# Linear recurrence stage: gate weights multiplied with the input weights beforehand, phases counted in turns, sums made by TensorE, all in two halves

## The reference, cut to what matters

```python
def _L2_attn_a_ref(x, w_in, b_in, w_gx, b_gx, w_ga, b_ga, a_real_param, a_imag_param, w_out, b_out):
    xh = x @ w_in + b_in                               # 128 -> 256 channels
    gate_x = sigmoid(_bdl(xh, w_gx, b_gx))             # block diagonal, 256 -> 128
    gate_a = sigmoid(_bdl(xh, w_ga, b_ga))
    log_a = -8.0 * gate_a * softplus(a_real_param)
    log_a_imag = a_imag_param * gate_a
    a = exp(complex(log_a, log_a_imag))
    xc = complex(xh[..., :128], xh[..., 128:])
    xc = gate_x * xc
    norm = sqrt(maximum(1.0 - exp(2.0 * log_a), 1e-06))
    xc = norm * xc
    h = associative_scan(h_t = a_t * h_{t-1} + xc_t)   # along the sequence
    y = concatenate([h.real, h.imag], -1) @ w_out + b_out
x = x + _L2_attn_a_ref(_layernorm(x), ...)
```

## Time and profile before

| | us |
|---|---|
| median of 3 runs | 2849.07 |
| lowest, highest | 2848.08, 2852.46 |
| the profiled execution's own time | 2850.44 |
| its span, first to last instruction | 2848.7 |
| busy: PE, DVE, ACT, POOL | 2286.7, 1795.9, 1416.0, 690.6 |
| mean granted TensorE clock (share of full speed) | 0.887 |
| this stage, first instruction to the next stage's first | 1896.04 to 2002.92 |

### The profile page before, as it was taken

One profiled execution on the slowest core, in us unless ns is written; L12 is line 12 of the kernel. 1 busy time (PEld: TensorE's weight loads), 2 busy tenths in 40 slices (PEclk: granted clock), 3 DMA queues, 4 the chain that ended last, 5 costly groups with the idle time before them and its releaser, 6 DMA issues. The chain is left out here.

```text
span 2848.7 us, 41029 instructions
## 1 busy us (share of the span) xinstructions
PE 2286.7 (80%) x14474; PEld 1486.8 (52%) x14474; DVE 1795.9 (63%) x4001; ACT 1416.0 (50%) x3610; POOL 690.6 (24%) x448
## 2 busy tenths in 40 slices
PE   7999998887988797898655878780777889698977
PEld 4555554563664365464335776340332667475647
DVE  4655555884874795794655664338346899546863
ACT  4444544673773585584531214652553766315750
POOL 0000000561650362461022430000000779123000
PEclk9999998999999998998867989895887999878996
DMA  1000001010100210110102320000000122100010
GB/s 44 9 10 11 11 11 61 22 27 16 23 20 5 75 24 12 27 24 8 46 9 53 73 51 17 11 11 0 6 13 32 60 75 74 63 10 1 2 62 16
DMA packets 79015, 80.17 MB, mean 28 GB/s; under 512 B 28624, under 2 KB 63952, under 8 KB 77808
## 3 DMA queue, kind: packets, MB, share of 16 engines
q1 hardware_dynamic: 78832, 77.80, 9.5%
HBM read 53.55 MB, written 8.52 MB: 22 GB/s over the span
## 5 line engine op out<-in xcount | busy, mean ns | idle before, releaser
L800 ACT ACTIVATE window_s<-window_s,window_soft 128x128 f32<-128x128 f32 x512 | 197.7, 394 | 5.0 <-DVE window_soft L963 5.0
L878 POOL TENSOR_TENSOR window_pa<-window_pa,window_pb 128x1024 f32<-128x1024 f32 x64 | 151.6, 2369 | 152.3 <-DVE window_pb L945 152.3
L870 POOL TENSOR_TENSOR window_s<-window_s,window_soft 128x512 f32<-128x512 f32 x128 | 133.2, 1041 | 219.8 <-DVE window_soft L900 219.6
L963 DVE CUSTOM_DVE_ANT_0 window_s<-ps,window_mask,window_nrn 128x128 f32<-128x128 f32 x512 | 148.5, 346 | 46.6 <-PE ps L645 29.9
L2854 DVE TENSOR_TENSOR_SCAN mamba_bx<-ps,mamba_ab 128x256 f32<-128x256 f32 x256 | 154.5, 667 | 18.8 <-PE ps L2640 18.8
L608 PE MATMUL ps<-window_wa,window_sh 128*128 128x512 f32 x256 | 132.1, 641 | 41.6 <-DVE window_pb L945 29.0
L861 POOL MEMSET window_sh<- 64x2048 f32 x2 | 3.6, 1800 | 569.8 <-POOLq L53 569.8
L3024 ACT ACTIVATE rope_p<-ps,rope_mx 128x128 f32<-128x128 f32 (+1 forms) x256 | 104.3, 419 | 48.7 <-DVE rope_mx L3078 48.7
L2637 PE MATMUL ps<-mamba_m,mamba_xt 128*128 128x129 f32 x512 | 103.0, 283 | 29.4 <-ACT mamba_m L2712 20.6
L100 ACT ACTIVATE ln_sq<-ps 128x512 f32<-128x512 f32 x120 | 71.5, 597 | 106.1 <-PE ps L83 105.3
L83 PE MATMUL ps<-x,consts 128*128 128x512 f32 x128 | 84.4, 821 | 49.4 <-PEq L53 38.2
(11 more groups left out here) (577 smaller groups left out, 6235.1 us busy)
## 6 DMA issues: line engine op xcount, KB each, us to landing
mamba_cbr<-mamba_c SPq DMA_DIRECT2D x32, 512.0 KB, 3.6
window_vs<-window_vt SPq DMA_DIRECT2D x64, 128.0 KB, 2.3
delta_xi<-delta_x SPq DMA_DIRECT2D x16, 512.0 KB, 4.7
switch_w<-in_switch_w SPq DMA_DIRECT2D x4, 2048.0 KB, 10.2
window_wa<-in_window_wa SPq DMA_DIRECT2D x4, 1152.0 KB, 7.3
linattn_wb<-in_linattn_wb SPq DMA_DIRECT2D x6, 513.0 KB, 3.5
window_wb<-in_window_wb SPq DMA_DIRECT2D x4, 537.5 KB, 8.2
window_sh<-y SPq DMA_DIRECT2D x16, 128.0 KB, 2.2
```

Source lines behind the costliest of these rows:

```text
L800: a = nc.scalar.activation(s[:, k % 2, e, c, :], s[:, k % 2, e, c, :], ACT.Exp, scale=-1.0, bias=soft[:, k % 2, e, 1, c:c + 1], accum_out= ...
L870: nc.gpsimd.tensor_tensor(s[:, k % 2, e], s[:, k % 2, e], soft[:, k % 2, e, 3, :].unsqueeze(2).to_broadcast([P, QC, P]), ALU.mult)\
L878: nc.gpsimd.tensor_tensor(own, own, pb[:, :, :, :].rearrange("p a h d -> p (a h d)"), ALU.add)\
L963: v = nc.vector.tensor_tensor_reduce(s[:, k % 2, e, c, :], K.ps[:, B_S + e, toks(c, P)], mask[:, k % 2, :], nrn[:, k % 4, h:h + 1], 3e38, ...
```

## The change

It rewrites `lru_stage` and nothing else.

- **Composed gate weights.** TensorE transposes `win`, VectorE copies the result to SBUF (`winT`), TensorE multiplies it with the gates' weights, ScalarE copies the products (`comp`). The gates are then one matmul of `h` with `comp` for each tile. `remainder(i)` (not shown) waits for `e2` and makes `1 - nrm`, clipped from below, in two VectorE passes. The gates' biases get `gates_w.T @ b_in` added (four matmuls of one column and one VectorE sum). `xh` stays in PSUM; VectorE adds `b_in` as it multiplies by the gate.
- **Phases in turns.** ScalarE makes `ga * a_imag / 2 pi`; after the scan, two VectorE passes leave the phase's fraction. The cosine is a sine of `pi/2 - 2 pi |fraction|`, made by ScalarE.
- **Sums by TensorE.** The sums of products of both rotations are left to TensorE: before the scan by matmuls with the identity and its negative into PSUM, which the scan then reads; after it by giving all four products to the output matmul, one with negated weights.
- **Two halves.** Passes over 2048 columns become two over 1024.

```diff
+            for c in range(2):
+                mm = nc.tensor.transpose(K.ps[:, 4, toks(c, P)], win[c], K.ident)
+            mm.then_inc(st.win_turned, 1)
+            pe.wait_ge(outer.log_ready, 3)
+            for g in range(2):
                 for c in range(2):
+                    mm = nc.tensor.matmul(K.ps[:, 6, g:g + 1], gates_w[g][c], b_in[c], start=(c == 0), stop=(c == 1))
+            mm.then_inc(st.shift_ready, 1)
+            pe.wait_ge(st.win_moved, 1)
+            for g in range(2):
+                for c in range(2):
+                    mm = nc.tensor.matmul(K.ps[:, 5, toks(g, P)], winT[:, toks(c, P)], gates_w[g][c],
+                                          start=(c == 0), stop=(c == 1))
+            mm.then_inc(st.comp_ready, 1)
+            pe.wait_ge(st.comp_moved, 1)
...
+            for j in range(NJ):
+                pe.wait_ge(outer.norm_ready, j + 1)
+                if j == 2:
+                    pe.wait_ge(st.gate_bias, 1)
+                nc.tensor.matmul(K.ps[:, 4 + j, :], comp[:, toks(1, P)], K.h[:, toks(j)], start=True, stop=True)\
+                    .then_inc(st.ga_ready, 1)
+            for j in range(NJ):
+                nc.tensor.matmul(K.ps[:, j, :], comp[:, toks(0, P)], K.h[:, toks(j)], start=True, stop=True)\
+                    .then_inc(st.gx_ready, 1)
+            for c in (1, 0):
+                for j in range(NJ):
+                    pe.wait_ge((st.gx_done, st.ga_done)[c], j + 1)
                     nc.tensor.matmul(K.ps[:, 4 * c + j, :], win[c], K.h[:, toks(j)], start=True, stop=True)\
                         .then_inc(st.xh_ready, 1)
-            for j in range(NJ):
-                pe.wait_ge(st.xh_done, 2 * j + 2)
-                for g in range(2):
-                    for c in range(2):
-                        mm = nc.tensor.matmul(K.ps[:, 4 * g + j, :], gates_w[g][c], xh[:, c, toks(j)],
-                                              start=(c == 0), stop=(c == 1))
...
+            def total(i):
                 for c in range(2):
+                    pe.wait_ge(st.xn, 2 * (i + 1))
+                    for n in range(2):
+                        pe.wait_ge(st.rot, 4 * i + 2 * c + n + 1)
+                        for j in (2 * i, 2 * i + 1):
+                            mm = nc.tensor.matmul(K.ps[:, 4 * c + j, :], (K.ident, nident[:, :])[c * n],
+                                                  parts[2 * c + n][:, toks(j)], start=(n == 0), stop=(n == 1))
+                    mm.then_inc(st.summed, 1)
+
+            def output(i):
+                for n, w in enumerate((wout[0], nwout[:, :], wout[1], wout[1])):
+                    pe.wait_ge(st.prod, 4 * i + n + 1)
+                    for j in (2 * i, 2 * i + 1):
+                        mm = nc.tensor.matmul(K.ps[:, j, :], w, prods[n][:, toks(j)], start=(n == 0), stop=(n == 3))
+                        if n == 3:
+                            mm.then_inc(st.out_ready, 1)
+
+            total(0)
+            total(1)
+            output(0)
+            output(1)
...
+            act.wait_ge(st.comp_ready, 1)
+            nc.scalar.activation(comp[:, :], K.ps[:, 5, 0:2 * P], ACT.Copy).then_inc(st.comp_moved, 1)
...
+            for j in range(NJ):
+                act.wait_ge(st.ga_ready, j + 1)
+                nc.scalar.activation(ga[:, toks(j)], K.ps[:, 4 + j, :], ACT.Sigmoid, bias=bias[:, 1:2])\
+                    .then_inc(st.ga_done, 1)
+            act.wait_ge(st.consts, 1)
+            for i in range(2):
+                act.wait_ge(st.ga_done, 2 * (i + 1))
+                nc.scalar.activation(tn[:, half(i)], ga[:, half(i)], ACT.Identity, scale=turn).then_inc(st.turns, 1)
...
+            for i in range(2):
+                act.wait_ge(st.om, 2 * (i + 1))
+                nc.scalar.activation(nrm[:, half(i)], nrm[:, half(i)], ACT.Ln).then_inc(st.norm_log, 1)
+                act.wait_ge(st.norm_log, i + 1)
+                nc.scalar.activation(nrm[:, half(i)], nrm[:, half(i)], ACT.Exp, scale=0.5).then_inc(st.norm_done, 1)
+            for i in range(2):
+                act.wait_ge(st.frac, i + 1)
+                nc.scalar.activation(sn[:, half(i)], ph[:, half(i)], ACT.Sin, scale=-2 * PI_IN).then_inc(st.sin_done, 1)
+                act.wait_ge(st.r_done, 2)
+                nc.scalar.activation(ab[:, half(i)], ph[:, half(i)], ACT.Abs).then_inc(st.abs_done, 1)
+                act.wait_ge(st.abs_done, i + 1)
+                nc.scalar.activation(cs[:, half(i)], ab[:, half(i)], ACT.Sin, scale=-2 * PI_IN, bias=quarter)\
+                    .then_inc(st.cos_done, 1)
...
+            dve.wait_ge(st.win_turned, 1)
+            nc.vector.tensor_copy(winT[:, :], K.ps[:, 4, 0:2 * P]).then_inc(st.win_moved, 1)
             outer.dve(dve, 0, K.h)
+            dve.wait_ge(st.shift_ready, 1)
+            nc.vector.tensor_tensor(bias[:, :], K.ps[:, 6, 0:2], wt[:, 1026:1028], ALU.add).then_inc(st.gate_bias, 1)
...
+            def phases(i):
+                dve.wait_ge(st.turns, i + 1)
...
+                nc.vector.tensor_scalar(tn[:, half(i)], ph[:, half(i)], ROUND, None, ALU.add).then_inc(st.rounded, 1)
...
+                nc.vector.scalar_tensor_tensor(ph[:, half(i)], tn[:, half(i)], ROUND, ph[:, half(i)],
+                                               ALU.subtract, ALU.subtract).then_inc(st.frac, 1)
...
+            def inputs(i):
+                dve.wait_ge(st.norm_done, i + 1)
+                dve.wait_ge(st.gx_done, NJ)
+                nc.vector.tensor_tensor(gx[:, half(i)], gx[:, half(i)], nrm[:, half(i)], ALU.mult).then_inc(st.gated, 1)
+                dve.wait_ge(st.gated, i + 1)
+                dve.wait_ge(st.xh_ready, 2 * NJ)
+                for c in range(2):
+                    for j in (2 * i, 2 * i + 1):
+                        v = nc.vector.scalar_tensor_tensor(xh[:, c, toks(j)], K.ps[:, 4 * c + j, :], b_in[c],
+                                                           gx[:, toks(j)], ALU.add, ALU.mult)
+                    v.then_inc(st.xn, 1)
+
+            def rotate(i):
...
+                for n, (a, c) in enumerate(((cs, 0), (sn, 1), (cs, 1), (sn, 0))):
+                    nc.vector.tensor_tensor(parts[n][:, half(i)], a[:, half(i)], xh[:, c, half(i)], ALU.mult)\
+                        .then_inc(st.rot, 1)
+
+            def scan(i):
+                dve.wait_ge(st.masked, 1)
+                for c, to in enumerate((hr, hi)):
+                    dve.wait_ge(st.summed, 2 * i + c + 1)
+                    src = K.ps[:, 4 * c + 2 * i:4 * c + 2 * i + 2, :].rearrange("p b n -> p (b n)")
+                    nc.vector.tensor_tensor_scan(to[:, half(i)], r[:, half(i)], src, 0.0, ALU.mult, ALU.add)\
+                        .then_inc(st.scanned, 1)
+
+            def back(i):
+                dve.wait_ge(st.scanned, 2 * (i + 1))
+                for n, (a, h) in enumerate(((cs, hr), (sn, hi), (sn, hr), (cs, hi))):
+                    nc.vector.tensor_tensor(prods[n][:, half(i)], a[:, half(i)], h[:, half(i)], ALU.mult)\
+                        .then_inc(st.prod, 1)
+
+            phases(0)
+            phases(1)
+            remainder(0)
+            remainder(1)
...
+            inputs(0)
+            inputs(1)
+            rotate(0)
+            rotate(1)
+            scan(0)
+            back(0)
+            scan(1)
+            back(1)
```

160 lines of the change are left out of this document (53 added, 107 removed).

## The result

The changed kernel takes 2817.06 us (median; 2813.15 to 2818.59), the kernel before 2848.95 (2848.08 to 2852.46): a ratio of 0.9884, 95% interval 0.9867 to 0.9901. The forecast was 2812.8 with a range of 2807 to 2820, so the time lies in the range, 4.3 us above the forecast.

What follows compares the result with a forecast made beforehand. The stage's end was taken as set by TensorE, then VectorE's list, then TensorE again. Gains of 13.3 (head), 18.1 (body) and 5.0 (tail) make 36.4, taken as 36.3, giving a median of 2812.8 us, range 2807 to 2820.

Steps and rivals of the forecast that it cites:

- Head: From the stage's begin to VectorE's first phase scan: start at 1913.6 instead of 1926.87, a gain of 13.3 us.
- the normed tiles: In the head, four LayerNorm tiles queue on VectorE behind the `winT` copy: done at 1908.2, 0.3 later than `rstd` would allow.
- eight one-column records: In the head, the small matmuls for the gates' biases, sized at 0.117 us a record and hidden beside the normed tiles.
- Table load: ScalarE's sigmoid table in the head: 1.28 us by the trace; the skill page's extra 1.38 would make the gain 34.9.
- Body: VectorE's list from phases to back products: 47.5 us instead of 65.6, ending at 1961.1, a gain of 18.1 us.
- low clock in the sums: TensorE's sums for half 0 start slow, costing 1.8 us; they still lie hidden with 1.5 us to spare.
- Tail: From VectorE's end to the stage's last add: 4.5 us instead of 9.5, a gain of 5.0 us.
- Later stages: Unchanged stages behind the rewritten one: no term in the sum, 3 us to either side for meeting TensorE's clock at other moments.
- early low clock: Rival: TensorE's clock falls in the head, slowing small records and gate matmuls; all moves by 3.4 us, 2816; chance 0.14.
- low clock in sums and outputs: Rival: TensorE stays at 1.2 GHz from 1935 on; last add 25 us later than forecast, 2838; chance 0.08.
- The slower case: Rival: low clock plus exposed weight loads in the new tail; stage ends about 9 us later than before, 2858; chance 0.03.

Runs made afterwards that it cites:

- gates as before: The changed kernel with the input matmuls, ScalarE's bias pass, sixteen gate matmuls and all sigmoids ahead of the turns put back: stage 85.01 us against 71.35, whole 2827.93.
- the second trace: The changed kernel run again unaltered, timed against the kernel before: median 2819.03 us against 2851.77, ratio 0.9881; its later stages take 850.27 us.

## Why the prediction was right, and what it missed

- **Head: right.** Forecast start 1913.6, measured 1911.05 + 2.51 = 1913.56; gain 13.3. Its steps hold as well: the copy of `winT` 0.42 (0.45 taken), the normed tiles done at 1907.94 on that clock (1908.2), eight one-column records in 1.05 us, 0.13 each, near the 0.12 taken. That the sum hits to 0.04 us is in part luck: the table load ended 0.15 later than taken (1910.05, 1909.9), and the four sigmoids took 2.42 us where four times 0.63 were taken, a price that the earlier trace rows does not show. The gates as before cost 13.7 in the experiment.
- **Table load: the row was right.** The sigmoid's load lasts 1.28 us from 1906.26 and the first sigmoid begins at 1907.56, 0.02 behind it. The Trainium skill, ScalarE: Activation LUTs, section What ACT_TABLE_LOAD costs, adds 1.38 of drain; the measurement decides, and shows none.
- **Body: right.** The list ends at 1961.06 on the clock of before (1961.1), with one wait of 0.86 (0.8) ahead of the gated inputs. The sums lie hidden, but not with 1.5 us to spare: the term *low clock in the sums* was 1.8 and measured 9.85 - 6.87 = 2.98 (the second half's eight matmuls take 6.87 at full clock, 1942.35 to 1949.22). The row that I had sized it by, TensorE's start in the earlier trace rows, has 2.9 us of half clock, the sums after 13.45 us of idling here 5.9.
- **Tail: 0.85 short.** Forecast 4.5 us behind VectorE, measured 5.35. (The terms as written add up to 1965.45, not 1965.6; that is 0.15 of slip to the other side.) I let the second half's output begin with its first product; it began 0.94 later, behind the sums' lost 1.2 us. With the clock raised ahead of the sums this 0.94 went away. So the stage's sum was 36.3 and measured 35.5.
- **Later stages: the larger miss.** I gave them zero with 3 us to either side and read that from the scatter of the runs. They are no scatter: -1.0, -0.5, -2.9, +2.5, +1.8, +3.2 and +0.3 us in the order of the table, +3.4 in sum, and +4.6 in the second trace. They are also more than the 3 us allowed. Together with the tail that is about the 4.3 us by which the median lies above the forecast; the four executions spread over 5.4 us, so that it fits to 0.1 is luck. So is part of the margin: the second median, 2819.03, lies 1.0 under the range's upper end.
- **Rivals.** The early low clock did not come: the small records and the gates (3.70 us for eight records) ran at full clock. The low clock in sums and outputs came for the first 6 us alone; from 1938.92 on TensorE ran at full clock with a backlog, as the argument against it had said. The slower case did not come: the change of weights after every second matmul stays hidden (1.72 us from one pair to the next).

The gain is not one part's. Taking back the gates, the halves or the sums costs 13.7, 13.9 and 10.9 us, 38.5 together against 35.5. The fourth part, the phases in turns, was not taken back in a run; by the rows, angles, scan and rounding took 14.44 us before (1926.87 to 1941.31) and 8.67 after (1911.05 to 1919.72), 5.77 less. So the four do not add up to the gain; that they overlap in the waits which each takes away is argued, not shown.

## What to carry to other kernels

Cutting a long chain of passes in halves can pay without removing any work: the price is some fixed costs, the gain is every wait in which another engine's turn stood on the path. Sums of products given to an otherwise idle TensorE pay if it then stays busy to the end; a few useless matmuls ahead of a burst are worth a try where it starts at half clock (0.9 us in the stage here, nothing in the whole). A gain under about 5 us in one stage of a long kernel should be read in the stage, since the stages behind it can move by as much or more.

## What the hardware showed beyond that

- Later stages of unchanged code took 840.2 to 854.3 us in all, depending on what the stage ahead of them did; two traces of the kernel before agreed within 0.02 us in six of the seven stages.
- In the rotary stage a stretch of half clock 10.2 us longer (27.27 against 17.07) went with 3.2 us more, with no instruction changed.
- A pause on TensorE of 0.07 to 1.07 us stood behind 11537 to 11539 matmul records in all fourteen traces: it moved by six records within its stage when six were added in the program half a millisecond earlier. Where it fell 7 to 16 records into its line, switch 1 took 97.12 to 98.07 us, where it fell 63 or 64 in, 96.15 to 96.23.
- A scan of 1024 columns from PSUM comes every 2.20 us (1949.42 to 1951.62), or 2.33 where its sum was only just there (1940.22 to 1942.55); the one from SBUF was taken at 2.25.
